# Neighbourhood attention on one Trainium2 core: softmax weights as two fp16 parts, transposed together and spread by one fp16 matmul a neighbour

## What is computed

```python
x = x + layernorm(attn(layernorm(x)))
x = x + layernorm(ffn(layernorm(x)))       # GRU of 512 steps that routes 8 experts; untouched

# attn, with K = 13, NS = 6, HEADS = 16, HEAD_DIM = 8
q, k, v = qkv[0] * SCALE, qkv[1], qkv[2]
ni = clip(i - NS, 0, L - K)                # first neighbour of token i
kg, vg = k[:, :, nbr, :], v[:, :, nbr, :]
attn = einsum('bhld,bhlkd->bhlk', q, kg) + rpb[:, bidx]
attn = softmax(attn, axis=-1)
out = einsum('bhlk,bhlkd->bhld', attn, vg)
return out @ proj_w.T + proj_b
```

## Time and profile before

| | us |
|---|---|
| median of 3 runs | 4211.66 |
| lowest and highest | 4198.45, 4226.81 |
| the profiled execution | 4216.87 |
| its span | 4215.0 |
| PE busy, of the span | 3881.9 (92%) |
| VectorE busy | 3103.6 (74%) |
| ScalarE busy | 1509.4 (36%) |
| mean granted clock | 0.977 |
| spread matmuls (L511), 208 records, sum of their times | 116.9 |
| start of L395, eight times | 93.44, 153.52, 196.46, 239.38, 284.31, 328.91, 373.53, 416.53 |

### The profile page before, as it was taken

The page is one execution under the profiler, slowest core; times in us unless marked ns, Lnnn a source line. Parts: engine busy times, 40 slices in busy tenths (PEclk is TensorE's granted clock), DMA queues, the critical chain, the costliest instruction groups (busy, mean ns, idle before and its releaser), DMA issues. The chain is left out here.

```text
span 4215.0 us, 179359 instructions
## 1 busy us (share of the span) xinstructions
PE 3881.9 (92%) x76838; PEld 2507.1 (59%) x76838; DVE 3103.6 (74%) x14963; ACT 1509.4 (36%) x5111; POOL 161.7 (4%) x399
## 2 busy tenths in 40 slices
PE   3999589999999999999999999999999999987999
PEld 3777455656665666566665665656666656654665
DVE  2688677777777777777777777777777777776555
ACT  1112333333333444333333333333333334432222
POOL 1221000000000000000000000000000000000000
PEclk9899789999999999999999999999999999988999
DMA  2010400000000000000000000000000000010000
GB/s 67 18 37 35 155 3 3 3 3 3 3 3 3 3 3 3 3 3 3 3 3 3 3 3 3 3 3 3 3 3 3 3 3 3 3 36 8 10 10 12
DMA packets 46472, 51.44 MB, mean 12 GB/s; under 512 B 11668, under 2 KB 39572, under 8 KB 45716
## 3 DMA queue, kind: packets, MB, share of 16 engines
q1 hardware_dynamic: 45716, 40.48, 3.1%
HBM read 36.28 MB, written 4.19 MB: 10 GB/s over the span
## 5 line engine op out<-in xcount | busy, mean ns | idle before, releaser
L886 PE MATMUL psum<-room,h_parts 128*32 128x384 f16 x65536 | 2770.7, 327 | 137.5 <-DVE h_parts L1015 137.5
L886 PEld LDWEIGHTS psum<-room,h_parts 128*32 128x32 f16 x65536 | 1663.9, 97 | 1161.0 <-DVE h_parts L1015 359.9
L971 DVE STREAM_TRANSPOSE turned<-psum 128x128 f32<-128x128 f32 x1024 | 323.6, 316 | 524.2 <-PE psum L886 524.2
L1075 ACT ACTIVATE r_by<-gates 128x32 f32<-128x32 f32 x1024 | 253.2, 247 | 1154.3 <-DVE gates L950 1154.3
L747 DVE CUSTOM_DVE_ANT_0 products<-routes 128x128 f32<-128x128 f32 x1855 | 478.4, 270 | 5.0 <-ACT routes L740 3.0
L998 DVE TENSOR_TENSOR_SCAN state<-w_by,state 128x96 f32<-128x96 f32 x1024 | 366.4, 358 | 129.3 <-ACT state L1081 0.7
L1084 ACT ACTIVATE state<-state 128x32 f32<-128x32 f32 x1024 | 255.3, 249 | 434.7 <-DVE state L998 434.7
L989 DVE TENSOR_TENSOR_SCAN pre_n<-r_by,n_terms 128x96 f32<-128x96 f32 x1024 | 366.5, 358 | 22.9 <-ACT r_by L1075 2.3
L950 DVE TENSOR_TENSOR gates<-turned 128x32 f32<-128x32 f32 x2048 | 375.2, 183 | 0.0
L981 DVE STREAM_TRANSPOSE n_terms<-psum 128x128 f32<-128x128 f32 x1024 | 332.6, 325 | 0.0
L1081 ACT ACTIVATE state<-pre_n 128x32 f32<-128x32 f32 x1024 | 258.7, 253 | 136.6 <-DVE pre_n L989 3.4
(11 more groups left out here) (157 smaller groups left out, 2661.5 us busy)
## 6 DMA issues: line engine op xcount, KB each, us to landing
xs_room<-in_L_ffn_gru_w_hh_dram SPq DMA_DIRECT2D x16, 1536.0 KB, 7.1
room<-in_L_attn_x_dram SPq DMA_DIRECT2D x8, 256.0 KB, 5.4
x_scratch<-room SPq DMA_DIRECT2D x8, 256.0 KB, 2.3
room<-x_scratch SPq DMA_DIRECT2D x32, 64.0 KB, 2.2
out_dram<-room SPq DMA_DIRECT2D x32, 64.0 KB, 2.0
xs_room<-in_L_ffn_gru_w_ih_dram SPq DMA_DIRECT2D x3, 512.0 KB, 5.5
xs_room<-in_L_ffn_gate_w_dram SPq DMA_DIRECT2D x2, 512.0 KB, 6.1
xs_room<-in_L_ffn_up_w_dram SPq DMA_DIRECT2D x2, 512.0 KB, 4.5
```

Of the source, the lines that this page charges most:

```text
L886: last = nc.tensor.matmul(psum[32 * j:32 * j + 32, bank_of(k, half), 0:3 * P], h_parts[:, q, c, :], w_hh_s[:, s, half, 4 * c + j, :, :].re ...
L971: nc.vector.transpose(turned[:, half, 0, :], gate_bank(k, half, 0)).then_inc(r_turned[half], 1)
```

## The change

The normalised weights are scaled by 4096 (the factor goes into the inverse of the sum) and split: ScalarE converts them to fp16 (`prob_parts[..., 0, :]`, semaphore `probs_hi`), VectorE subtracts that from the fp32 weights to a second fp16 part (`prob_parts[..., 1, :]`, semaphore `probs_lo`). Both parts of a neighbour stand side by side, so that 4 neighbours x 2 parts x 16 heads fill 128 rows; 13 neighbours make 4 groups (`NGRP`), the last of 32 rows. The transposes are fp16, 16 instead of 8. The spread matmul has 1/4096 in place of one, adds both parts in one fp16 matmul, and still has 512 columns. `x2` gets a tile of its own, and the fp16 identity is made in the first block.

```diff
-        spread = sb("spread", [P, P // HEADS, P])
+        spread = sb("spread", [P, 4, P], F16)
...
-        pT = [carve(L), carve(L)]
+        NGRP = (K + 3) // 4
+        prob_parts = carve(TPS * K * HEADS).bitcast(F16).rearrange("p (t k s h) -> p t k s h", t=TPS, k=K, s=2)
+        pT = carve(NGRP * L // 2).bitcast(F16).rearrange("p (g l) -> p g l", g=NGRP)
         att = carve(TPS, C)
-        x2 = carve(TPS, C)
+        x2 = sb("x2", [P, TPS, C])[:, :, :]
...
+        pT_bank = [psum[:, b, :].bitcast(F16).rearrange("p (g l) -> p g l", g=2) for b in (PT_BANK, T_BANK)]
...
+                        nc.vector.tensor_scalar(total[:, :, :], total[:, :, :], PSCALE, None, ALU.mult)
+                        dve.drain()
                         nc.vector.tensor_tensor(probs, probs, total[:, :, :].unsqueeze(2).to_broadcast([P, TPS, K, HEADS]),
                                                 ALU.mult).then_inc(probs_done, 1)
                     value_product(11)
+                    if has_s:
+                        dve.wait_ge(probs_hi, s + 1)
+                        nc.vector.tensor_tensor(prob_parts[:, :, :, 1, :], probs, prob_parts[:, :, :, 0, :], ALU.subtract).then_inc(probs_lo, 1)
                     value_product(12)
...
+                    if present(s):
+                        act.wait_ge(probs_done, s + 1)
+                        nc.scalar.copy(prob_parts[:, :, :, 0, :], probs).then_inc(probs_hi, 1)
                     if present(c):
                         act.wait_ge(xn2T_ps, c + 1)
...
-                        nc.scalar.copy(pT[0], psum[:, PT_BANK, :])
-                        nc.scalar.copy(pT[1][0:WIN - P, :], psum[0:WIN - P, T_BANK, :]).then_inc(pT_done, 1)
+                        nc.scalar.copy(pT[:, 0:2, :], pT_bank[0])
+                        nc.scalar.copy(pT[:, 2, :], pT_bank[1][:, 0, :])
+                        nc.scalar.copy(pT[0:2 * HEADS, 3, :], pT_bank[1][0:2 * HEADS, 1, :]).then_inc(pT_done, 1)
...
-                            half, rows = (0, P) if j < P // HEADS else (1, WIN - P)
-                            nc.tensor.matmul(psum[:, j % 3, :], spread[0:rows, j % (P // HEADS), :], pT[half][0:rows, :],
+                            rows = 2 * HEADS * min(4, K - j // 4 * 4)
+                            nc.tensor.matmul(psum[:, j % 3, :], spread[0:rows, j % 4, :], pT[0:rows, j // 4, :],
                                              start=True, stop=True).then_inc(spread_ps, 1)
...
                     project(10)
+                    project(11)
                     if has_s:
-                        pe.wait_ge(probs_done, s + 1)
+                        pe.wait_ge(probs_lo, s + 1)
                         if present(c):
                             pe.wait_ge(xn2T_done, c + 1)
...
-                            row = probs[:, t, :, :].rearrange("p k h -> p (k h)")
-                            nc.tensor.transpose(psum[:, PT_BANK, t * P:(t + 1) * P], row[:, 0:P], ident[:, :])
-                            last = nc.tensor.transpose(psum[0:WIN - P, T_BANK, t * P:(t + 1) * P], row[:, P:WIN], ident[:, :])
+                            row = prob_parts[:, t, :, :, :].rearrange("p k s h -> p (k s h)")
+                            for g in range(NGRP):
+                                at, end = g * P, min((g + 1) * P, 2 * WIN)
+                                last = nc.tensor.transpose(pT_bank[g // 2][0:end - at, g % 2, t * P:(t + 1) * P], row[:, at:end], ident_16[:, :])
                         last.then_inc(pT_ps, 1)
-                    project(11)
                     project(12)
```

More of the change, by code:

```diff
@@ L40, in sandwich @@
     EPS = 1e-5
+    PSCALE = 4096.0
     assert C == P and B * 4 == 32 and G == NEXP * P and GM == 8
@@ L83, in sandwich @@
         ident = sb("ident", [P, P])
+        ident_16 = sb("ident_16", [P, P], F16)
         head_of = sb("head_of", [P, HEADS])
-        spread = sb("spread", [P, P // HEADS, P])
+        spread = sb("spread", [P, 4, P], F16)
         bias_win = sb("bias_win", [P, TPS, HEADS, K])
@@ L110, in sandwich @@
         consts = sem("consts")
+        spread_hi = sem("spread_hi")
         raw_in = [sem("raw_in0"), sem("raw_in1")]
@@ L151, in _ @@
                 nc.gpsimd.memset(spread[:, :, :], 0.0).then_inc(zeroed, 1)
+                nc.gpsimd.memset(ident_16[:, :], 0.0).then_inc(zeroed, 1)
                 nc.gpsimd.memset(head_of[:, :], 1.0).then_inc(zeroed, 1)
                 nc.gpsimd.memset(eps[:, :], EPS)
-                pool.wait_ge(zeroed, 3)
+                pool.wait_ge(zeroed, 4)
                 nc.gpsimd.affine_select(out=ident[:, :], in_=ident[:, :], compare_op=ALU.not_equal, fill=1.0,
                                         base=0, pattern=[[-1, P]], channel_multiplier=1).then_inc(consts, 1)
+                nc.gpsimd.affine_select(out=ident_16[:, :], in_=ident_16[:, :], compare_op=ALU.not_equal, fill=1.0,
+                                        base=0, pattern=[[-1, P]], channel_multiplier=1).then_inc(consts, 1)
                 sv = spread[:, :, :].rearrange("p j (h d) -> p j h d", h=HEADS)
-                nc.gpsimd.affine_select(out=sv, in_=sv, compare_op=ALU.not_equal, fill=1.0, base=0,
-                                        pattern=[[-HEADS, P // HEADS], [-1, HEADS], [0, HD]],
+                nc.gpsimd.affine_select(out=sv, in_=sv, compare_op=ALU.not_equal, fill=1.0 / PSCALE, base=0,
+                                        pattern=[[-2 * HEADS, 4], [-1, HEADS], [0, HD]],
+                                        channel_multiplier=1).then_inc(spread_hi, 1)
+                pool.wait_ge(spread_hi, 1)
+                nc.gpsimd.affine_select(out=sv, in_=sv, compare_op=ALU.not_equal, fill=1.0 / PSCALE, base=-HEADS,
+                                        pattern=[[-2 * HEADS, 4], [-1, HEADS], [0, HD]],
                                         channel_multiplier=1).then_inc(consts, 1)
@@ L164, in _ @@
                                         base=0, pattern=[[-HD, HEADS]], channel_multiplier=1).then_inc(consts, 1)
-                pool.wait_ge(consts, 3)
+                pool.wait_ge(consts, 4)
                 nc.gpsimd.affine_select(out=head_of[:, :], in_=head_of[:, :], compare_op=ALU.is_ge, fill=0.0,
@@ L243, in sandwich @@
         probs_done = sem("probs_done")
+        probs_hi = sem("probs_hi")
+        probs_lo = sem("probs_lo")
         pT_ps = sem("pT_ps")
@@ L677, in sandwich @@
         history = sb("history", [P, CH, 2, SP_T, B], F16)
-        ident_16 = sb("ident_16", [P, P], F16)
         x_tile = sb("x_tile", [P, P])
@@ L773, in _ @@
                 nc.gpsimd.memset(w_by[:, :, :, 1], 1.0).then_inc(cleared, 1)
-                nc.gpsimd.tensor_copy(ident_16[:, :], ident[:, :])
                 pool.wait_ge(h0_top, 1)
```

## The result

| | before | after |
|---|---|---|
| median | 4212.27 | 4294.74 |
| lowest and highest | 4198.45, 4226.81 | 4281.11, 4302.72 |
| runs | 4 | 4 |
| the profiled execution | 4216.87 | 4302.72 |
| mean granted clock | 0.977 | 0.953 |

The medians lie 82 us apart. The profiled execution is the slowest of the four after the change, and 21.6 us above the fastest. The forecast was 4242, in a range up to 4280. By the profiled executions, which the prediction summed against, it is 4302.7 - 4216.9 = 85.8 us.

A forecast was written before the change was run, and what follows sets the result against it. PE was taken as the nearer limit, VectorE close behind, with the clock deciding. Four fallen steps of 55.9 us and three of 42 (+26.5), with the ends +25.5, on 4216.9 gave 4242, range 4205 to 4280.

The forecast's parts named there:

- The spread and the groups: In the scores: fp16 spread 0.23 us at full clock, 0.46 at half; PE's repeated projection-spread-scores group 2.91 and 5.58.
- A fall after the 24 records stays until the scores are done: After the densest score matmuls, 24 records of 16 columns each, half clock lasts through that step's scores: 8.5 us more.
- So four stretches of seven fall: Of seven stretches between softmax normalisations, four fall to half clock: 4 x 55.9 + 3 x 42 = 349.6, 26.5 us more.
- The step of 55.9 us: A fallen attention step: 44.93 us plus 8.5 for half-clock groups, 2.3 for later keys, 0.2 for scaling.
- The tail, P + 12.35: From P, the end of the normalisation, key products start at P + 12.35 against P + 10.0: 2.3 us later each step.
- The transposes were put at "nothing": In the softmax tail: sixteen fp16 transposes at 0.057 us take 0.91 us, against 0.9 for eight fp32 ones.
- Steps that are not caught: 42 us: Attention steps at full clock: VectorE sets the pace at 40.6 us, a half-clock dip adds 1 to 2; 42 against 42.9.
- B: Rival: all seven attention steps fall, since shorter groups leave PE idle and falls needn't await the 24 records; +67, 4284; chance 0.12.
- C: Rival: in the attention steps the clock recovers and PE leaves the path; 7 x 42, -30 us, 4187; chance 0.15.
- D: Rival: half and full clock alternate in a fallen step's groups, 49.2 us a step; 4216, no change; chance 0.13.
- The value-only step and the ends: Attention's values-alone step takes about 20 us, 3.5 less than 23.55; last softmax tail adds 2.3, the first 0.2.
- The rule on transposes: In the tail: if transposes don't count as busy, a further fall in three better steps adds some 5 us.

The follow-up runs named there:

- the idle matmuls in the kernel with one part: Kernel before with fp16 spread of the high part only, plus idle fp16 matmuls after each neighbour's scores: 4188.02 us, ratio 0.9942.
- the one with its spreads and the longer tail: Kernel before with conversion, subtraction, PE's wait and the eleventh projection moved ahead; fp32 transposes and spreads kept: 4242.35 us, ratio 1.0076.
- the spread with the waits: Kernel before with fp16 spread of the high part only, plus conversion, subtraction and PE's wait for them: 4261.19 us, ratio 1.0098.
- the kernel with two spreads and one part: Kernel before with fp16 spread of the high part only, every spread issued twice: 4196.49 us, ratio 0.9954.
- with and without the copies: Kernel before with high-part fp16 spread, conversion, subtraction and wait: 1.0098 without, 1.0132 (4262.94 us) with two more ScalarE copies of 512 columns.

## Why the prediction was wrong

The side was right, and so were the place and what a fallen step looks like. How many steps fall was not, and the size was off by 60 us in the profiled executions (+85.8 measured, +25.5 forecast). By its own steps:

- **The spread and the groups.** Forecast 0.23 and 0.46 us, groups of 2.91 and 5.58. Measured 0.215 at full clock (0.86 over four) and 0.43 at half; the group at half clock is 5.54. Right. The Trainium skill, "TensorE: Matmul & The Clock Gate", section "Wait — 56ns, not 53.3ns?", gives 215.7 and 426.7 ns for such a matmul at the two clocks; the trace agrees. The group at full clock, in the kernel with the short spread alone, is 278.23 - 275.34 = 2.89.
- **A fall after the 24 records stays until the scores are done.** Right: half clock starts in the records at 170.55 and again in those at 229.01, and lasts 30.7 to 34.1 us. That the thinner work behind the records has to do with it is shown by the four spreads and by the idle matmuls in the kernel with one part: none caught. Wide spreads make it rarer and don't exclude it: the kernel before has one caught stretch of seven, and so has the one with its spreads and the longer tail.
- **"So four stretches of seven fall."** This is the step that failed. Seven fell, in the execution shown. Three more at 59.0, their mean, in place of 42 are 51.0 of the 63.3 us by which the seven stretches missed the forecast (412.9 against 349.6). The reason given was that nothing in the change touches the 24 records, so that the three batches that passed before would pass again. The short spread alone did give four, the spread with the waits five, and the whole change seven, each in one execution, and the last in the slowest of its four. What stands around the records counts as well as the records, as the idle pairs between them and the repeated spreads show, and the count in one profile of the kernel before was no property of the kernel: its own runs range over 4192 to 4240 on one chip.
- **The step of 55.9 us.** Measured 58.9 in the step shown. The 24 records themselves are partly at half clock, 173.83 - 170.55 = 3.28 against 2.59, which is 0.7; the tail gives 2.1; 0.2 is spread out. By the mean of 59.0 it is 3.1, and with four stretches 12.4, the rest of the 63.3.
- **The tail, P + 12.35.** Measured P + 14.5 in the step shown, with P = 212.15. Conversion, subtraction and their waits were right to 0.02 us: the transposes start at P + 2.07 (forecast 2.05), though at P + 2.59 in four of the eight tails. The transposes were put at "nothing", P + 3.1 at their end; ScalarE has them at 216.91, P + 4.76, since 0.057 us holds only between like shapes and the clock is at half from 213.6. That is 1.7 us. The shapes alone have a good part of it: at full clock the sixteen took 1.79 us in this order and 1.16 in that by group. The copies took 1.96, 0.4 less than forecast. From the value projection to the first key product it is 7.74 us against 6.92, as the projection at 218.92 runs at half clock: 0.8. So a fall in the tail, which the prediction allowed for the kernel of now and priced at 1 to 2 us in the 42, belonged in the caught steps too.
- **Steps that are not caught: 42 us.** No step of the changed kernel was free. With the short spread alone they take 41.2 to 41.8, where the sum without the tail's 2.3 would have had about 40 (37.2 busy, 1 of drains, 1 to 2 for a dip). With the whole tail they take 44.1 to 48.2 (two spreads) and 47.4 to 48.3 (four, after the first), both with more work on PE, so three free stretches would probably have been worse than forecast too.
- **Rivals.** By its own sign, at least six steps that fall, it is B that came (chance 0.12), and it has the nearest time, 4284. Its reason was not shown: it had falls begin in any group, since PE idles, and in the trace all seven long falls begin in the 24 records or right behind them. C and D did not happen in the changed kernel. D's swings, short stretches of half clock within the groups, are seen in the kernel with two spreads and one part (13.7 us, steps of 48.8). The sign of being wrong, half clock in every step, is the one that was met.
- **The value-only step and the ends.** The rest of the program gives 4.0 us back, where the forecast had 1.0 (3.5 less, then 2.3 and 0.2 more). The step with values alone takes 20.8 us against 23.55, 2.8 less; the last tail is 1.8 longer, and the first normalisation starts 0.6 later, so the ends give 0.4. The other 3.5 or so lie behind the attention, and no run says why. The 63.3 of the seven stretches less these 3.0 are the 60 us of the miss. Constants and `x2` cost nothing that can be seen.
- **The rule on transposes.** It would have brought a further fall in the tail. There is one now, at 213.6, but PE had idled for 2.98 us until 212.87, and the transposes start at 214.22, so it speaks neither for the rule nor against it.

What stays open: why seven of seven are caught by the whole change. A longer tail alone doesn't do it (five of seven, with and without the copies), and the sixteen transposes in whichever order leave it at seven in the executions shown. But a profile holds one execution. Both counts of seven are from the slowest of four, and one five from the second fastest of seven, so a part of the difference, perhaps most, is the choice of execution; the medians (ratios of 1.0098, 1.0132 and 1.0177) are the better measure, and their intervals overlap or nearly do. That a further wait or load before the 24 records shifts how the clock stands when they come is only argued, and no run here tests it.

## What to carry to other kernels

A change that shortens PE's work can cost more through the clock than it saves: ask for each shortened matmul what will keep PE dense once the clock has fallen, and price a step at both clocks before counting how often it falls. The count in one profile is an observation with a wide spread, not a constant: put the case "every step" into the sum as if it were likely wherever one step of several is caught already. Where PE has slack against another engine, a pair of idle matmuls in the thinnest place is a cheap test and, at times, the cure; and a split into two parts is best made where it lies behind the work on the path (here after the transposes), not in front of it.

## What the runs showed of the hardware

- Half clock holds on with PE busy nearly all the time: 33.58 of 34.10 us and 34.10 of 34.10 in the two stretches above. Busy time by the records did not bring the clock back; kernels that added wider matmuls to the same records did not stay there. The Trainium skill, "TensorE: Matmul & The Clock Gate", section "HAM oscillation — how this bites in real kernels", puts the loss down to idle gaps while PE waits; the case there is another, and in these stretches there was hardly a gap.
- Useless matmuls made a program faster: 4231 to 4188 us. Each spread matmul issued four times took the changed kernel from 1.0177 to 1.0052.
- At full clock fp16 transposes of changing shape (128 and 32 rows) start 148 to 163 ns apart, like shapes of 128 rows 55 to 56, and 66 right behind a change.
- The same instructions in the same program take 41.2 or 53.7 us a step within one execution (short spread alone).
